# Turning u in 32x32 blocks on VectorE instead of whole on TensorE

## The reference

```python
x = x + xattn(layernorm(x), ctx, lens, Wq, Wk, Wv, Wo, q_norm_w, k_norm_w)   # 16 heads of 64
x = x + attn(layernorm(x), w_qkv, w_out)                                     # causal, 64 latents of a batch
x = x + ffn(layernorm(x), w_gate, w_up, w_down)                              # quantized values
# in xattn: keys and queries are RMS-normalized per head, keys past lens[b] are masked,
# attn = softmax(q k / 8);  o = attn v;  out = o Wo
```

## Time and profile before

| | us |
|---|---|
| median of 3 runs | 2695.4 (2695.36 to 2696.43) |
| the profiled execution | 2697.39 |
| its span, first to last instruction | 2695.6 |

### The profile page before, as it was taken

How to read it: one execution, slowest core, us unless ns; L and a number is a source line. 1 busy time by engine, 2 the same in 40 slices (tenths; PEclk the granted TensorE clock), 3 DMA queues, 4 the chain that set the end, 5 groups by cost and what they waited for, 6 DMA issues and landing times. The chain is left out here.

```text
span 2695.6 us, 53614 instructions
## 1 busy us (share of the span) xinstructions
PE 2469.7 (92%) x16223; PEld 2103.9 (78%) x16223; DVE 2084.8 (77%) x3036; ACT 1369.4 (51%) x3017; POOL 1198.7 (44%) x620
## 2 busy tenths in 40 slices
PE   6879999999999999999999999999999867899842
PEld 3657888888888888888888888888888766677612
DVE  6689888888888888888888888888888722566467
ACT  5634555555555555555555555555555320566530
POOL 3403555555555555545555555555555300122245
PEclk8999999999999999999999999999999979999975
DMA  2321111111111111111111111111111045000000
GB/s 87 154 98 42 56 51 56 49 50 60 49 51 54 49 49 48 48 48 56 56 49 49 61 49 49 56 49 49 49 48 44 29 161 175 1 0 0 1 0 16
DMA packets 141694, 144.53 MB, mean 54 GB/s; under 512 B 10520, under 2 KB 120272, under 8 KB 141520
## 3 DMA queue, kind: packets, MB, share of 16 engines
q1 hardware_dynamic: 137040, 127.16, 14.9%
q10 hardware_dynamic: 4608, 16.78, 1.5%
HBM read 109.17 MB, written 34.73 MB: 53 GB/s over the span
## 5 line engine op out<-in xcount | busy, mean ns | idle before, releaser
L382 POOL TENSOR_TENSOR probs<-scores,best_all 128x1024 f32 (+2 forms) x398 | 944.5, 2376 | 919.3 <-DVE best L734 919.3
L937 PEld LDWEIGHTS u_ps<-rows,probs 128*128 128x128 f32 x6656 | 806.5, 192 | 47.0 <-issue 5.3
L937 PE MATMUL u_ps<-rows,probs 128*128 (+1 forms) x6656 | 810.1, 275 | 9.0 <-ACT probs L575 6.6
L719 DVE SCALAR_TENSOR_TENSOR scores<-s_ps,mask,rrms 128x512 f32 (+2 forms) x832 | 619.0, 745 | 249.3 <-PE s_ps L806 249.0
L575 ACT ACTIVATE probs<-probs 128x1024 f32<-128x1024 f32 (+1 forms) x416 | 439.6, 1058 | 512.0 <-POOL probs L382 500.8
L528 ACT ACTIVATE squares<-k_ps 128x512 f32<-128x512 f32 (+1 forms) x832 | 463.2, 595 | 191.8 <-PE k_ps L806 132.5
L695 DVE TENSOR_REDUCE ssq<-squares 128x16 f32<-128x1024 f32 (+1 forms) x416 | 502.6, 1208 | 0.0
L734 DVE TENSOR_TENSOR best<-best,scores 128x1024 f32<-128x1024 f32 (+1 forms) x352 | 469.0, 1332 | 0.3
L804 PE MATMUL k_ps<-w_hi,cT_hi 128*128 128x512 f32 (+1 forms) x832 | 363.3, 437 | 12.9 <-DVE cT_lo L689 12.9
L804 PE MATMUL s_ps<-q_hi,cT_hi 128*128 (+2 forms) x832 | 361.9, 435 | 2.5 <-ACT uT_sb L554 1.4
L806 PE MATMUL s_ps<-q_hi,cT_lo 128*128 (+2 forms) x832 | 327.7, 394 | 0.0
(11 more groups left out here) (206 smaller groups left out, 2502.4 us busy)
## 6 DMA issues: line engine op xcount, KB each, us to landing
stage<-in_ctx SPq DMA_DIRECT2D x384, 64.0 KB, 1.8
rows<-in_ctx SPq DMA_DIRECT2D x32, 768.0 KB
queries<-probs SPq DMA_DIRECT2D x16, 1024.0 KB, 4.0
q_plain<-queries SPq DMA_DIRECT2D x32, 512.0 KB, 3.3
u_transposed<-uT_sb ACTq DMA_DIRECT2D x32, 512.0 KB, 2.7
a_uT<-u_transposed SPq DMA_DIRECT2D x16, 1024.0 KB, 4.8
best_all<-best_rows SPq DMA_DIRECT2D x31, 512.0 KB, 3.6
a_wqkv<-in_L_attn_w_qkv SPq DMA_DIRECT2D x1, 1536.0 KB, 9.1
```

What stands on the lines that cost most here:

```text
L382: pool.tensor_tensor(probs[0:r, slot_of(c, PRING), :], scores_at(b, c), best_all[0:r, bass.ds((b % 2) * HL, HL)], ALU.subtract).then_inc(s ...
L719: dve.scalar_tensor_tensor(out=scores_at(p, c, h * HALF, HALF).rearrange("p (h l) -> p h l", l=L), in0=s_ps[h][0:r, :].rearrange("p (h l) ...
L937: last = pe.matmul(u_ps[g // 3][:, at:at + UW], probs[0:r, s, g * P:(g + 1) * P], rows, start=(c == 0 and g % 3 == 0), stop=(c == NC - 1), ...
```

## The change

VectorE's `transpose` of a 128x256 part turns each 32x32 block within itself: partition 32 q + k and column 32 c + i of a group swap only k and i. Four of them, one at the end of each of VectorE's steps 7 to 10 (`turn_u`), turn `u_sb` into `uT_sb`. After that partition 32 q + i of `uT_sb` holds, for each group g and each c, the 32 elements of rows 128 g + 32 q + k and width 32 c + i. Four DMA stores, one for each q, put them in place in the same DRAM layout: each reads 32 partitions and writes 32 x 8 x 4 = 1024 runs of 32 elements (128 bytes). ScalarE issues them at the start of step 11 (`store_uT`), before its exponential. TensorE's eight transposes, ScalarE's two evictions and the waits on them stay for the last batch alone (`turn_last_u`, `save_last_uT`, `store_last_uT`; `ending(p)`), with semaphores of their own. `divide` now waits for VectorE's turns of the batch before, and VectorE's first turn for the stores of the batch before.

```diff
--- before.py
+++ after.py
@@ -108,6 +108,11 @@
     return isinstance(p, int) and p >= B
 
 
+def ending(p):
+
+    return isinstance(p, int) and p == B + 1
+
+
 class On:
 
 
@@ -129,6 +134,7 @@
 
 
 LAG = 6
+SIDE = 32
 CREDIT = 2 * NC
 TURN_AHEAD = NC - 1
 KEYS_AHEAD = NC - 2
@@ -252,7 +258,7 @@
         q_stored = [sem(f"q_stored{s}") for s in range(2)]
         q_hi_ready, q_ready = Turns(sem("q_hi_ready"), 2), Turns(sem("q_ready"), 2)
         stage_in = [sem(f"stage_in{s}") for s in range(RING + 1)]
-        q_in, rows_in, ut_stored = sem("q_in"), sem("rows_in"), Turns(sem("ut_stored"), 1, 16)
+        q_in, rows_in, ut_stored = sem("q_in"), sem("rows_in"), Turns(sem("ut_stored"), 1, 64)
 
         turned = Turns(sem("turned"), CREDIT)
         hi_ready = Turns(sem("cT_hi_ready"), CREDIT)
@@ -281,8 +287,8 @@
         last_spread, last_best_ready = sem("last_spread"), sem("last_best_ready")
         inv_ready = Turns(sem("inv_ready"), 2, 3)
         u_ready = Turns(sem("u_ready"), 2, 3)
-        u_turned = Turns(sem("u_turned"), 2, 2)
-        uT_ready = Turns(sem("uT_ready"), 2, 2)
+        last_u_turned, last_uT_ready, last_ut_stored = sem("last_u_turned"), sem("last_uT_ready"), sem("last_ut_stored")
+        uT_ready = Turns(sem("uT_ready"), 2, 4)
         block = ctx.enter_context(nc.Block())
 
         def half(h):
@@ -367,7 +373,8 @@
             for j in range(1, TILES // CHUNK):
                 load_x(j)
             each_step(sp, query, step, KEYS_FROM - 4)
-            sp.wait_ge(ut_stored.sem, ut_stored.ended(B - 1))
+            sp.wait_ge(ut_stored.sem, ut_stored.ended(B - 2))
+            sp.wait_ge(last_ut_stored, 16)
 
         @block.gpsimd
         def _(pool):
@@ -540,6 +547,7 @@
                                    ACT.Copy).then_inc(last_best_ready, 1)
 
             def divide(b):
+                act.wait_ge(uT_ready.sem, uT_ready.ended(b - 1))
                 for k in range(3):
                     act.wait_ge(inv_ready.sem, inv_ready.ended(b, k + 1))
                     for g in range(3 * k, min(3 * k + 3, G)):
@@ -548,15 +556,23 @@
                                               scale=inv_sum[:, g:g + 1])
                     last.then_inc(u_ready.sem, 1)
 
-            def save_uT(b, h):
-                act.wait_ge(u_turned.sem, u_turned.ended(b, h + 1))
-                act.wait_ge(ut_stored.sem, ut_stored.ended(b - 1))
-                act.activation(uT_sb[:, half(h)], x_ps[:, :], ACT.Copy).then_inc(uT_ready.sem, 1)
-
             def store_uT(b):
                 act.wait_ge(uT_ready.sem, uT_ready.ended(b))
-                act.dma_start(ut_out[bass.ds(b, 1), :, :].rearrange("b d n -> (b d) n"),
-                              uT_sb[:, :]).then_inc(ut_stored.sem, 16)
+                dest = ut_out[bass.ds(b, 1), :, :].rearrange("b (c i) (g q k) -> b q i g c k", i=SIDE, k=SIDE, q=P // SIDE)
+                for q in range(P // SIDE):
+                    act.dma_start(dest[:, q, :, :, :, :].rearrange("b i g c k -> (b i) g c k"),
+                                  uT_sb[q * SIDE:(q + 1) * SIDE, :].rearrange("i (g c k) -> i g c k", k=SIDE, c=D // SIDE)
+                                  ).then_inc(ut_stored.sem, 16)
+
+            def save_last_uT(b, h):
+                if h == 0:
+                    act.wait_ge(ut_stored.sem, ut_stored.ended(b - 1))
+                act.wait_ge(last_u_turned, h + 1)
+                act.activation(uT_sb[:, half(h)], x_ps[:, :], ACT.Copy).then_inc(last_uT_ready, 1)
+
+            def store_last_uT(b):
+                act.wait_ge(last_uT_ready, 2)
+                act.dma_start(ut_out[b, :, :], uT_sb[:, :]).then_inc(last_ut_stored, 16)
 
             def step(p, c, on):
                 n = p * NC + c
@@ -564,10 +580,12 @@
                     save_row(p - 1)
                 if on.rows and c == 2 and draining(p):
                     save_last_best(p - 1)
-                if on.finish and c in (LAG + 2, LAG + 3):
-                    save_uT(p - 2, c - LAG - 2)
-                if on.finish and c == LAG + 4:
+                if on.finish and c == LAG + 5 and not ending(p):
                     store_uT(p - 2)
+                if c in (LAG + 2, LAG + 3) and ending(p):
+                    save_last_uT(p - 2, c - LAG - 2)
+                if c == LAG + 4 and ending(p):
+                    store_last_uT(p - 2)
                 if on.values:
                     act.wait_ge(shifted.sem, shifted.ended(n - NC - LAG))
                     vc = (c - LAG) % NC
@@ -588,8 +606,8 @@
                     rough_rrms(p, 1)
 
             act.preload_act_table_set(EXP_LN)
-            for turns in (hi_ready, squared, logged, y0_ready, probs_ready, row_saved, u_ready, uT_ready,
-                          ut_stored, q_hi_ready):
+            for turns in (hi_ready, squared, logged, y0_ready, probs_ready, row_saved, u_ready, ut_stored,
+                          q_hi_ready):
                 turns.start(act)
             rough_layernorm(0)
             act.wait_ge(qkw_ready, 1)
@@ -738,6 +756,13 @@
                 turned_best = s_ps[h] if draining(b + 1) else x_ps
                 dve.tensor_reduce(best_row[:, 4 * h:4 * h + 4], turned_best[:, :].rearrange("p (g s) -> p g s", s=P),
                                   AX_X, ALU.max).then_inc(best_row_ready.sem, 1)
+
+            def turn_u(b, k):
+                if k == 0:
+                    dve.wait_ge(u_ready.sem, u_ready.ended(b))
+                    dve.wait_ge(ut_stored.sem, ut_stored.ended(b - 1))
+                cols = slice(k * HL // 4, (k + 1) * HL // 4)
+                dve.transpose(uT_sb[:, cols], u_sb[:, cols]).then_inc(uT_ready.sem, 1)
 
             def invert_sums(b):
                 dve.wait_ge(valued.sem, valued.ended(b * NC + NC - 1))
@@ -778,6 +803,8 @@
                     scale(p, n, c, 1)
                 if on.keys:
                     sum_squares(n + KEYS_AHEAD, at_step(p, c, KEYS_AHEAD)[1])
+                if on.finish and LAG < c <= LAG + 4 and not ending(p):
+                    turn_u(p - 2, c - LAG - 1)
                 if on.early and c == NC - 3:
                     mean_squares(p + 1, n + KEYS_AHEAD, 0)
                 if on.late and c == 1:
@@ -787,7 +814,7 @@
                 if on.late and c == 2:
                     refine_rrms(p, 1)
 
-            for turns in (lo_ready, summed, ms_ready, rrms_ready, scaled, kept, best_row_ready, inv_ready):
+            for turns in (lo_ready, summed, ms_ready, rrms_ready, scaled, kept, best_row_ready, inv_ready, uT_ready):
                 turns.start(dve)
             layernorm_variance(0)
             dve.wait_ge(norm_w_in, 64)
@@ -916,12 +943,12 @@
             def turn_row(b):
                 pe.transpose(x_ps[0:G, 0:P], best_row[:, :], ident[:, :]).then_inc(row_turned.sem, 1)
 
-            def turn_u(b, h):
+            def turn_last_u(b, h):
                 pe.wait_ge(u_ready.sem, u_ready.ended(b))
                 for g in range(4):
                     at = (4 * h + g) * P
                     last = pe.transpose(x_ps[:, g * P:(g + 1) * P], u_sb[:, at:at + P], ident[:, :])
-                last.then_inc(u_turned.sem, 1)
+                last.then_inc(last_u_turned, 1)
 
             def values(b, m, c):
                 s, r = slot_of(c, PRING), rows_of(c)
@@ -946,8 +973,8 @@
                     pe.wait_ge(best_row_ready.sem, best_row_ready.ended(p - 1, c))
                 if on.rows and c == 3 and not draining(p):
                     pe.wait_ge(row_saved.sem, row_saved.ended(p - 1))
-                if on.finish and c in (LAG + 2, LAG + 3):
-                    pe.wait_ge(uT_ready.sem, uT_ready.ended(p - 2, c - LAG - 1))
+                if c == LAG + 2 and ending(p):
+                    pe.wait_ge(last_uT_ready, 1)
                 if on.turn:
                     later, tile = at_step(p, c, TURN_AHEAD)
                     turn(later, n + TURN_AHEAD, tile)
@@ -956,7 +983,7 @@
                 if on.values:
                     vc = (c - LAG) % NC
                     values(p - 1 if c >= LAG else p - 2, n - NC - LAG, vc)
-                if (on.rows and c < 3) or (on.finish and c in (LAG + 1, LAG + 2)):
+                if (on.rows and c < 3) or (c in (LAG + 1, LAG + 2) and ending(p)):
                     pe.wait_ge(lo_ready.sem, lo_ready.ended(n + TURN_AHEAD if on.turn else B * NC - 1))
                 if on.rows and c in (0, 1) and not draining(p):
                     turn_best(p - 1, c)
@@ -968,10 +995,10 @@
                 if on.rows and c == 1 and draining(p):
                     pe.wait_ge(squared.sem, squared.ended(B * NC - 1))
                     spread_last_best(p - 1)
-                if on.finish and c in (LAG + 1, LAG + 2):
-                    turn_u(p - 2, c - LAG - 1)
-
-            for turns in (turned, keys, scored, valued, best_turned, row_turned, u_turned):
+                if c in (LAG + 1, LAG + 2) and ending(p):
+                    turn_last_u(p - 2, c - LAG - 1)
+
```

(1 more changed line is left out.)

## The result

The changed kernel takes 2853.66 us (median of 4 runs, 2848.83 to 2855.62) against 2695.55 before (median of 4): ratio 1.0583, 95% interval 1.0565 to 1.0602. The forecast was slower, but 2744 with a range of 2694 to 2815, so the time lies 39 us above the range. The profiled execution took 2848.83 us, span 2847.0, against 2697.39 and 2695.6. One run of the kernel that issues in four places took 5661 us, and nothing here explains it.

A forecast was written before the change was run, and what follows sets the result against it. TensorE's own queue was taken to bound the loop; a 2.5 us stall less 0.91 us won gives +1.6 us a batch, 48 us over 30 batches: 2743 to 2744 us in a timed run. Range 2694 to 2815.

The forecast's parts named there:

- the start of the issues: ScalarE's first store issue in step 11 at T + 1.3, after VectorE's fourth transpose; that transpose ready at T + 1.0 at earliest.
- the clock behind the gap: TensorE's clock after its wait in step 11: the sum ran on at 1.00 and added nothing for a fall.
- What bounds the loop; what is won: TensorE's own queue sets the loop's length; removing its eight transposes from steps 7 and 8 wins 0.91 us a batch.
- VectorE's turns: Four 128x256 block transposes ending VectorE's steps 7 to 10, 0.42 us each, bounds 0.31 and 0.84.
- T: Start of `project` on TensorE in step 11 of a pass; 1065.31 us in the pass the prediction read.
- The issues: ScalarE's four store issues in step 11: first at T + 1.3, fourth accepted at T + 4.2.
- The reading of the earlier trace: A DMA queue holds about 128 pieces per engine; the fourth store is accepted when 64 pieces, 30 ns each, are out.
- rival 1: ScalarE's queue takes all four stores, only issues cost: stall 1.1 to 1.4 us, 2701 to 2710 us; chance 0.20.
- The gap: TensorE stands 2.5 us once a pass: `values` of step 11 at T + 5.5 in place of T + 2.98.
- The slack in front of `values` and the hand-over: In step 11: 0.8 us of slack before `values`, and 0.2 us allowed from the exponential's end to the matmul.
- Rival 2: Same backlog, but 58 ns a piece, or the stall lowers the clock, 1.5 us a pass: 2790 to 2845 us; chance 0.15.
- Faster (3): ScalarE's four issues overlap or cost under 0.2 us each, coverable by 3.18 us idle before the exponential: 2668 us; chance 0.12.

The follow-up runs named there:

- one plain store: Changed kernel, its four stores replaced by one of 128 unbroken 4 KB rows at the start of step 11, 32x32 blocks left unplaced: 2685.96 us, ratio 0.9969.
- early turns: Changed kernel with two block transposes in each of VectorE's steps 7 and 8, none in 9 and 10, stores unmoved: 2668.08 us, ratio 0.9902.
- 8 copies: Kernel before the change, with eight unread 128x128 ScalarE copies in front of step 11's exponential: 2720.92 us, ratio 1.009.
- four plain stores: Changed kernel, its four stores each of 32 unbroken 4 KB rows in the same place, 32x32 blocks left unplaced: 2759.5 us, ratio 1.0232.
- 16 copies: Kernel before the change, with sixteen unread 128x128 ScalarE copies in front of step 11's exponential: 2789.23 us, ratio 1.0344.
- 21 copies: Kernel before the change, with 21 unread 128x128 ScalarE copies in front of step 11's exponential: 2852.46 us, ratio 1.0588.

## Why the prediction was wrong

Two terms of the sum were too small, the start of the issues and their length, and one was missing, the clock behind the gap.

- **What bounds the loop; what is won.** Right. 0.91 us was forecast for steps 7 and 8, 0.88 is what they lost, and with SyncE issuing it is kept.
- **VectorE's turns.** 0.42 us forecast, 0.43 measured; they fit beside TensorE's work. But the place of the fourth was wrong. I had `uT_ready` at T + 1.3, and earlier at best, because a freer ScalarE would let `q_lo` end sooner. GpSimd takes its work in order: `q_lo` stands behind a shift (the subtraction of the maximum), the shift waits for the `keep_best` that opens VectorE's step 9, and that stands behind VectorE's first two turns. Before, on T of that pass:

```profile
...
1056.12 1.22 DVE L734 TENSOR_TENSOR best<-best,scores 128x1024 f32<-128x1024 f32 x1
...
1057.59 2.40 POOL L382 TENSOR_TENSOR probs<-scores,best_all 128x1024 f32 x1 [2.67 <-DVE best L734]
```

That is T - 9.19 and T - 7.72; now `keep_best` begins at T - 8.39 (1046.44) and the shift at T - 6.96 (1047.87). `q_lo` came right behind it at 1050.21, and the `keep_best` that opens step 10, held up until `q_lo` was over, ended at 1053.70; the turn of step 10 was done at T + 1.86 and the first issue began at T + 2.03. 0.7 us, all of it on the path.
- **The issues.** The term was 2.9 us (first issue to the fourth accepted) and measured 3.1, but for another reason: that the size came out was luck. The reading of the earlier trace rows, that a queue holds some 128 pieces per engine, plays no part here: a piece of 128 bytes costs 13 ns and not 30 (3.7% of 16 engines x 2847 us over the 129104 packets of ScalarE's queue), so 64 are out in 0.8 us; and the stores of 64 pieces of 2 KB, 4 per engine, issue no faster. For the loads of the earlier trace rows it was not tried and stays open. The term is four issues of 0.61 to 0.77 us, with some 0.16 of register work and pause between two. 0.34 to 0.40 was taken from rows of other forms; the row that pointed right was x's 0.86, which I had put into rival 1.
- **The gap.** With both, `values` is late by 3.46 us in place of 2.5. The slack in front of `values` and the hand-over held.
- **The clock: the step that failed most.** The sum ran on at clock 1.00 behind the gap. The fall costs 2.9 us in most passes, 77 us over 29 of them, more than the rest of the error. Rival 2 had it, with the right consequence of the gap, but at 1.5 us from one row of another stage and at a chance of 0.15 together with dearer pieces. The doubling of the price of a short piece did not come, and rival 2's range of 2790 to 2845, too, ends below the measured 2854.
- **Not forecast:** the passes that drain gain as well. From the last load of rows to the last store of u it is 79.6 us before and 72.2 with SyncE issuing, but also 72.1 with the one plain store and 72.7 with the early turns, in both of which ScalarE issues as in the change. So it goes with the turns' leaving TensorE and not with the stores' leaving ScalarE; the change itself, with falls of the clock there too, has 77.7. I had counted nothing there.
- **Rivals.** Faster (3) was wrong about the change as made, but right that this idle time of ScalarE can cover the issues, once the turns are done in time: that is the kernel with early turns.

On the Trainium skill (DMA: Bandwidth & Descriptors, Specifications): its rule that pieces under 512 bytes cost a read-modify-write is not seen here as time. Pieces of 512 bytes, in the kernel with four dimensions, cost 39 ns (2.9% over 33872 packets), of 128 bytes 13 ns. Per byte that is 1.35 times as much. In the kernel with two stores of 128 rows a piece of 512 bytes took 29 ns, and against that it is 1.8 times.

## What to carry to other kernels

Work that costs nothing by busy time costs its full length once it runs past the idle time and the slack of an engine in whose order it stands in front of what the bounding engine waits for; put an issue behind the instruction that is waited for, or on a queue with nothing urgent behind it. Before counting on idle time, follow what makes the data ready through every engine in the chain, since an engine that takes its work in order passes a delay on from one job to the next. And when a gap of TensorE is in the forecast, price what follows it at the lower clock too, from a run with the gap made on purpose if there is one.

## What the runs showed of the hardware

The fall of the clock against TensorE's gap (its idle time before `values` of step 11), once a pass in a loop with TensorE otherwise busy all the time; 29 passes read in each kernel. Without a gap steps 11 and 12 together last 9.3 us.

| kernel | gap, us | steps 11 and 12 together, us (passes) |
|---|---|---|
| one plain store; 8 copies | 0.5 to 0.6 | no fall |
| two stores of 128 rows | 1.5 to 1.6 | no fall |
| four plain stores | 2.0 | 11.6 (15), 13.2 (14) |
| 16 copies | 2.35 | 12.0 (20), 13.6 (9) |
| pieces of 2 KB | 3.0 to 3.2 | 14.0 to 14.5 (20), 15.5 (9) |
| pieces of 512 bytes, four dimensions | 3.1 to 3.3 | 14.1 to 14.6 (16), 15.5 (13) |
| the change | 3.25 to 3.5 | 13.1 (1), 14.4 to 14.7 (3), 15.6 to 15.8 (25) |
| 21 copies | 3.5 | 13.1 (3), 14.7 to 14.8 (25), 15.9 (1) |

With four plain stores, 16 and 21 copies and the change, the first value is that of passes without a fall. A pass with one lasts 1.6 us more, the change's usual pass 2.6 more. So the clock fell or didn't fall behind the same gap from pass to pass, and it isn't told here what decides. Nor is 1.5 us safe elsewhere: while the pipeline drains in the kernel before, where TensorE has several gaps close together, the clock fell at 2147.9, just behind a gap of 1.28 us.

Two more:

- Two 128x256 block transposes in a row take VectorE 0.76 us.
- A block transpose was not held up by GpSimd's `q_lo`, which ran from 1050.21 to 1052.61 and held `keep_best` up: the transpose took 0.43 us from 1050.75, as it does elsewhere, and `keep_best` 2.59 from 1051.11 in place of 1.2.
